# Soft mixture of experts in one long kernel: combine weights transposed during the experts, and expert outputs stored by expert

## The reference

```python
xn = _l2norm(x, axis=2)
phin = scale * _l2norm(phi, axis=0)
logits = jnp.einsum('bmd,dnp->bmnp', xn, phin)
d = jax.nn.softmax(logits, axis=1)
c = jax.nn.softmax(logits.reshape(b_, m_, n_ * p_), axis=-1).reshape(b_, m_, n_, p_)
xs = jnp.einsum('bmd,bmnp->bnpd', xn, d)
h = jax.nn.gelu(jnp.einsum('bnpd,ndh->bnph', xs, w1) + b1[None, :, None, :], approximate=False)
ys = jnp.einsum('bnph,nhd->bnpd', h, w2) + b2[None, :, None, :]
y = jnp.einsum('bnpd,bmnp->bmd', ys, c)
```

## Time and profile before

| | us |
|---|---|
| median of 3 runs | 1000.62 |
| lowest, highest | 994.01, 1002.33 |
| span of the profiled execution | 1013.5 |
| experts on TensorE, first matmul to the last | 275.11 to 454.14 |
| combine on TensorE, first transpose to the last product | 460.00 to 493.96 |
| PE busy in the span | 878.3 (87%) |
| DVE, ACT, POOL busy | 460.6, 315.7, 279.8 |

### The profile page before, as it was taken

How to read it: one execution, slowest core, us unless ns; L and a number is a source line. 1 busy time by engine, 2 the same in 40 slices (tenths; PEclk the granted TensorE clock), 3 DMA queues, 4 the chain that set the end, 5 groups by cost and what they waited for, 6 DMA issues and landing times. The chain is left out here.

```text
span 1013.5 us, 18267 instructions
## 1 busy us (share of the span) xinstructions
PE 878.3 (87%) x6209; PEld 626.3 (62%) x6209; DVE 460.6 (45%) x1542; ACT 315.7 (31%) x904; POOL 279.8 (28%) x242
## 2 busy tenths in 40 slices
PE   6789999889999989886898899977465999999980
PEld 6677888666556545454654677756462666666650
DVE  5764555538533322226653588845681222222220
ACT  2444333227533222221231566633101122211210
POOL 1440000000000000000232355530018188888454
PEclk9999999779899999998995799985556999999995
DMA  8999000000079999963500000001105255555222
GB/s 246 256 296 420 5 2 2 1 1 1 2 301 421 420 420 421 421 242 101 195 8 1 1 2 1 0 1 27 48 15 144 65 102 103 101 105 92 37 24 23
DMA packets 64454, 128.52 MB, mean 127 GB/s; under 512 B 26910, under 2 KB 47184, under 8 KB 54912
## 3 DMA queue, kind: packets, MB, share of 16 engines
q1 hardware_dynamic: 34432, 118.22, 32.4%
q0 software_dynamic: 29952, 9.36, 6.9%
HBM read 115.37 MB, written 11.98 MB: 126 GB/s over the span
## 5 line engine op out<-in xcount | busy, mean ns | idle before, releaser
L1805 POOL DMA_INDIRECT out_dram<-yr,put x48 | 105.7, 2202 | 65.6 <-issue 43.7
L1259 POOL MEMSET xg<- 96x74 f32 x1 | 0.2, 157 | 420.1 <-PE bank L1233 420.1
L1869 PE MATMUL bank<-zTa,w 128*128 128x372 f32 x256 | 90.2, 497 | 0.8 <-DVE zTb L1943 0.8
L1791 POOL DMA_INDIRECT zr<-z_rows,take x48 | 66.5, 1386 | 85.9 <-issue 85.9
L1952 DVE TENSOR_TENSOR hT<-sg,bank 128x372 f32<-128x372 f32 x64 | 31.8, 539 | 107.6 <-ACT sg L1913 63.1
L1093 DVE COPY eh<-bank 128x384 f32<-128x384 f32 x32 | 17.8, 557 | 119.1 <-PE bank L1129 119.1
L1869 PEld LDWEIGHTS bank<-zTa,w 128*128 128x128 f32 x256 | 47.5, 194 | 38.2 <-ACT sg L1913 8.4
L1151 PE MATMUL bank<-w2s,eg 128*64 128x192 f32 x768 | 69.4, 330 | 0.0
L1883 PE MATMUL bank<-w2r,hT 128*124 128x192 f32 x384 | 66.1, 330 | 0.8 <-DVE hT L1952 0.8
L1883 PEld LDWEIGHTS bank<-w2r,hT 128*124 128x124 f32 x384 | 61.9, 187 | 3.8 <-issue 3.8
L1913 ACT ACTIVATE sg<-bank 128x372 f32<-128x372 f32 x64 | 27.3, 478 | 115.6 <-PE bank L1874 115.6
(11 more groups left out here) (287 smaller groups left out, 1766.0 us busy)
## 6 DMA issues: line engine op xcount, KB each, us to landing
w1s<-in_w_dram SPq DMA_DIRECT2D x32, 1152.0 KB, 12.7
w2s<-in_w_dram SPq DMA_DIRECT2D x32, 1152.0 KB, 14.8
w<-in_w_dram SPq DMA_DIRECT2D x8, 1024.0 KB, 7.8
xt<-in_x_dram SPq DMA_DIRECT2D x22, 336.0 KB, 9.1
xT<-in_xT_dram SPq DMA_DIRECT2D x22, 333.0 KB, 8.3
ys<-eo SPq DMA_DIRECT2D x64, 48.0 KB, 10.0
w2r<-in_w2r_dram SPq DMA_DIRECT2D x8, 384.0 KB, 4.7
e<-ys SPq DMA_DIRECT2D x21, 96.0 KB, 2.0
```

The costliest lines, as they stand in the source:

```text
L1791: nc.gpsimd.indirect_dma_start(zr[b][:, j, :], None, z_rows, bass.IndirectOffsetOnAxis(ap=take[:, k:k + 1], axis=0), bounds_check=NROW - 1 ...
L1805: nc.gpsimd.indirect_dma_start(rows_out, bass.IndirectOffsetOnAxis(ap=put[:, k:k + 1], axis=0), yr[e % 2][:, j, :], None, bounds_check=OUT ...
L1869: nc.tensor.matmul(bank[to + 2 * part + half][:, 0:HS], w13[b][:, 0, at:at + 128], zTa[b][:, half * HS:(half + 1) * HS], start=True, stop= ...
```

## The change

Four things are altered together.

1. Spreading, transposing and copying the combine weights moves from combine into the experts loop. In steps 2 to 23, TensorE has two transposes more (`transpose_c`) behind `hidden`, ACT a copy of 128 x 222 (`keep_c`) behind `copy_h`, and DVE the spreading (`spread_c`) behind the bias. The transposed weights of all tiles are kept in a new buffer `cT`. The transposes go to the unused columns 256 to 477 of banks 6 and 7, whose columns 0 to 191 hold expert outputs. Therefore `output(p)` for p below 22 now waits for `keep_c(p)`, and `transpose_c(t)` waits for ACT's copy of pair t - 2.
2. `ys` is ordered by expert. A store writes one block of 64 rows for an expert. To make a tile's rows reachable, image g * 21 + t now belongs to tile t as its g-th image in `xy`, which only changes where ACT's copy in dispatch writes.
3. Combine reads `ys` in ten DMAs: three for tiles 0 to 2, three for tiles 3 to 11, four for the rest, into two of the former weight buffers each for `e1` and `e2`. The bias `b2` is laid out twelve times by the host and loaded in two DMAs that SP issues in its step 33, between the stores of pairs 28 and 29.
4. Combine on TensorE is the 22 times two products alone, over four PSUM banks, written out without a loop; DVE has the addition of tile t and then the statistics of tile t - 1; ACT has nothing.

```diff
@@ experts_act
+            def keep_c(t):
+                act.wait_ge(s_eT, t + 1)
+                nc.scalar.copy(cT[:, t], bank[6 + t % 2][:, 256:256 + 2 * TP].rearrange("p (c q) -> p c q", c=2)).then_inc(s_eTa, 1)
+
             for s in range(NPAIR + 2):
                 if s < NPAIR:
                     copy_h(s)
+                if 2 <= s < T + 2:
+                    keep_c(s - 2)
                 if 0 <= s - 1 < NPAIR:
                     gelu(s - 1)
@@ experts_pe
                 pe.wait_ge(s_dg, p + 1)
-                if p >= 2:
+                if p < T:
+                    pe.wait_ge(s_eTa, p + 1)
+                elif p >= 2:
                     pe.wait_ge(s_do, p - 1)
...
+            def transpose_c(t):
+                b = t % 2
+                pe.wait_ge(s_ecw, t + 1)
+                if t >= 2:
+                    pe.wait_ge(s_do, t - 1)
+                spread = cw[b][:].rearrange("p g n -> p (g n)")
+                nc.tensor.transpose(bank[6 + b][:, 256:256 + TP], spread[:, 0:128], ident[0:TP, 0:TP])
+                nc.tensor.transpose(bank[6 + b][:, 256 + TP:256 + 2 * TP], spread[:, 128:4 * NE], ident[0:TP, 0:TP]).then_inc(s_eT, 1)
+
@@ experts_sp
-                        sp.dma_start(ys_of[:, p + e * NPAIR, :], eo[b][e * B:(e + 1) * B]).then_inc(s_eo[b], 16)
+                        sp.dma_start(ys_of[p + e * NPAIR], eo[b][e * B:(e + 1) * B]).then_inc(s_eo[b], 16)
+                if s == NPAIR + 1:
+                    sp.wait_ge(s_dh, NPAIR - 1)
+                    for k in range(2):
+                        sp.dma_start(e2[k][NE:2 * NE], ins["b2"].rearrange("n (t d) -> n t d", d=ED)).then_inc(s_b2, 16)
@@ combine_sp
+            for k, (lo, hi) in enumerate(LOADS):
+                to = slice(lo % EB, lo % EB + hi - lo)
+                for g in range(2):
+                    sp.dma_start(e1[lo // EB][g * NE:(g + 1) * NE, to], rows(g, lo, hi)).then_inc(s_el[k], 16)
+                sp.dma_start(e2[lo // EB][0:NE, to], rows(2, lo, hi)).then_inc(s_el[k], 16)
+                if hi == T - 1:
+                    sp.dma_start(e1[1][0:NE, hi % EB], ys_of[:, B - 1, :]).then_inc(s_el[k], 16)
@@ combine_pe
+            def product(t):
+                k = [lo <= t < hi or t == hi == T - 1 for lo, hi in LOADS].index(True)
+                pe.wait_ge(s_el[k], 64 if k == len(LOADS) - 1 else 48)
+                if t >= 4:
+                    pe.wait_ge(s_h, 2 * T + t - 3)
+                else:
+                    pe.wait_ge(s_dc[t % 2], NPAIR)
+                nc.tensor.matmul(bank[t % 4][0:TP, 0:ED], cT[:, t, 0], e1[t // EB][:, t % EB, :], start=True, stop=False)
+                nc.tensor.matmul(bank[t % 4][0:TP, 0:ED], cT[:, t, 1], e2[t // EB][:, t % EB, :], start=False, stop=True).then_inc(s_ey, 1)
```

More of the change, by code:

```diff
@@ L46 @@
 PAIR = 2 * TP
+EB = 12
+LOADS = ((0, 3), (3, EB), (EB, T - 1))
 EX, EH = 8, 512
@@ L255, in tower @@
         cw = [sb(f"cw{b}", [TP, GB + 1, NE]) for b in range(2)]
-        e1 = [sb(f"e1{q}", [128, ED]) for q in range(4)]
-        e2 = [sb(f"e2{q}", [128, ED]) for q in range(4)]
-        c1 = [sb(f"c1{b}", [128, TP]) for b in range(2)]
-        c2 = [sb(f"c2{b}", [128, TP]) for b in range(2)]
+        cT = sb("cT", [128, T, 2, TP])
+        e1 = [w1s[q][:].rearrange("p (t d) -> p t d", d=ED) for q in (2, 3)]
+        e2 = [w1s[q][:].rearrange("p (t d) -> p t d", d=ED) for q in (4, 0)]
         close_scope()
@@ L426, in tower @@
         s_cxc = sem("expert_input_stored")
-        s_w1 = [sem(f"w1_in_then_expert_rows_in{q}") for q in range(RING)]
-        n_w1 = [16 * len(range(q, NPAIR, RING)) for q in range(RING)]
+        s_w1 = [sem(f"w1_in{q}") for q in range(RING)]
         s_w2 = [sem(f"w2_in{q}") for q in range(RING)]
@@ L438, in tower @@
         s_eT = sem("combine_transposed")
-        s_eTa = sem("combine_copied_act")
-        s_eTd = sem("combine_copied_dve")
+        s_eTa = sem("combine_weights_kept")
+        s_b2 = sem("expert_output_bias_in")
+        s_el = [sem(f"expert_rows_in{k}") for k in range(len(LOADS))]
         s_ey = sem("combine_product")
@@ L902, in store @@
                 for c in range(2):
-                    n = B - t * GB if isinstance(t, int) and t == T - 1 else GB
-                    last = nc.scalar.copy(xy[:, c, :, bass.ds(t * GB, n)].rearrange("p n g -> p g n"), p[:, c, 0:n])
+                    if isinstance(t, int) and t == T - 1:
+                        last = nc.scalar.copy(xy[:, c, :, B - 1:B].rearrange("p n g -> p g n"), p[:, c, 0:1])
+                    else:
+                        to = xy[:, c, :, 0:B - 1].rearrange("p n (g t) -> p g n t", g=GB)
+                        last = nc.scalar.copy(to[:, :, :, bass.ds(t, 1)].rearrange("p g n o -> p g (n o)"), p[:, c])
                 last.then_inc(s_cxc, 1)
@@ L1163, in combine_sp @@
         def combine_sp(sp):
-            for q in range(4):
-                sp.dma_start(e2[q][NE:2 * NE], ins["b2"]).then_inc(s_cbi, 16)
             for b in range(2):
                 sp.wait_ge(s_eo[b], 16 * NPAIR)
-            def load(t, q):
-                if after(t, 4):
-                    sp.wait_ge(s_ey, t - 3)
-                first = t * GB * NE
-                if isinstance(t, int) and t == T - 1:
-                    sp.dma_start(e1[q][0:NE], ys[first:first + NE]).then_inc(s_w1[q], 16)
-                else:
-                    sp.dma_start(e1[q][:], ys[bass.ds(first, 2 * NE)]).then_inc(s_w1[q], 16)
-                    sp.dma_start(e2[q][0:NE], ys[bass.ds(first + 2 * NE, NE)]).then_inc(s_w1[q], 16)
@@ L1180, in combine_sp @@
[L1180 to L1203 removed]
+            rows = lambda g, lo, hi: ys_of[:, g * (T - 1) + lo:g * (T - 1) + hi, :]
@@ L1225, in product @@
-            def product(t, q):
-                b = q % 2
-                pe.wait_ge(s_eTa, t + 1)
-                pe.wait_ge(s_eTd, t + 1)
-                pe.wait_ge(s_w1[q], 8 * (t - q) + n_w1[q] + (16 if isinstance(t, int) and t == T - 1 else 32))
-                if after(t, 2):
-                    pe.wait_ge(s_h, 2 * T + t - 1)
-                nc.tensor.matmul(bank[b][0:TP, 0:ED], c1[b][:], e1[q][:], start=True, stop=False)
-                nc.tensor.matmul(bank[b][0:TP, 0:ED], c2[b][:], e2[q][:], start=False, stop=True).then_inc(s_ey, 1)
@@ L1238, in value_columns @@
+            for t in range(T):
+                product(t)
         def value_columns(j):
@@ L1995, in _ @@
             experts_act(act)
-            combine_act(act)
             near_act(act)
```

55 lines of the change are left out of this document (20 added, 35 removed).

## The result

The kernel after the change takes 997.06 us (median of 20 runs, 989.65 to 1007.5), the one before 1003.69 (20 runs, 994.01 to 1013.94): ratio 0.9948, 95% interval 0.9924 to 0.9973. That is 5 us faster, between 3 and 8, and outside the forecast range. The two medians are 6.6 us apart; the ratio leaves out the runs that lie more than 1.5% above the fastest of their kernel, and comes out nearer to 1. Over those 20 runs the kernel before stands 3 us above the median of the three runs that the prediction had.

The account below looks back on a forecast made before the run. Experts were bound by PE, later by DMA; combine by a ring of transposes, copies and products. Terms -14.4 - 0.6 + 0.4 = -14.6 us took 1000.62 to 986 us; forecast 982 to 990, 8-in-10 range 977 to 994.

Parts of the forecast that it names:

- The pitch: Combine's products: 0.71 us a tile at the higher clock, between 0.65 and 0.82; with the low-clock intervals, 14.4 us saved.
- Combine, its start: Store landing and first ys loads before combine: first product at 460.9 instead of 461.46, 0.6 us saved; no fourth-tile wait.
- The rest, at nothing: Other parts cost nothing: DVE's spreading, bias loads between stores 28 and 29, ACT's last copy, stores, dispatch copy, near.
- The clock at its start: Start of combine: some 5.5 us at the lower clock, four intervals of 1.28 us, then 17 of 0.71.
- Rival B: Loads run at half rate (210 GB/s), delaying the fourth tile and ACT's last copy: 991 us; chance 0.11.
- The experts: Experts loop: PE-bound steps grow to 5.3 to 5.4 us, 0.4 us lost; the DMA-bound part loses nothing.
- the DMA's pace comes later, near step 19: Experts loop: steps reach the DMA's 5.85 us pace near step 19 or 20 rather than 13.
- The added wait: DMA-bound experts steps: output matmuls wait for keep_c, PE opens the next step 0.6 us late, without accumulating; nothing lost.
- rival A: Experts: the load queue runs dry and the delay adds up, 6.57 us a step, 1002 us; chance 0.05.
- The clock elsewhere (C): Behind combine: work moved forward against the granted clock, up or down by 8, 978 or 994 us; chance 0.16.
- D: Combine: the clock does not rise, 21 intervals of 1.28 us, 995.7 us; chance 0.06 together with E.
- E: Rival: DVE and PE alternate in combine, 996 us; 0.06 with D. In "behind E": end of the experts' last output matmul.

Follow-up runs that it names:

- e5: Kernel after, with the two bias loads into 64 partitions replaced by one load of the same bytes into 128 (wrong bias): ratio 0.9939 to the kernel before.
- e2: Kernel after, with the two long bias loads replaced by one short load that GpSimd copies out: ratio 0.9866 to the kernel before.
- e10: e2 with ys read back in seven short stretches of tiles in place of three: 984.87 us, ratio 0.9807 to the kernel before.
- e1: Kernel after, with the ys loads for e1's rows going into 128 partitions instead of 64 (wrong rows): ratio 0.9935 to the kernel before.
- e4: Kernel after, with spreading, transposing and keeping the weights moved behind the experts, before the first product: ratio 0.9894 to the kernel before.
- e11: e2 with six short stretches and images reordered so two of three image groups load into 128 partitions: ratio 0.9827 to the kernel before.
- e12: e11 plus 14 matmuls that nothing reads, ahead of the first product: ratio 0.983 to the kernel before.
- e6: e2 plus 14 matmuls that nothing reads, ahead of the first product: ratio 0.9888 to the kernel before.
- e9: e6 plus 10 more matmuls that nothing reads, ahead of the fourth tile: ratio 0.9845 to the kernel before.

## Why the prediction was wrong

**The pitch was right.** At the high clock 0.65 us a tile (463.83, 464.48), where I took 0.71 between 0.65 and 0.82. DVE's two instructions overlap and keep the same 0.65.

**The step that failed is "Combine, its start" together with "The rest, at nothing".** There the sum took 254 to 420 GB/s for transfers of `ys`, 420 for the bias and no wait of the fourth tile, and ACT's last copy was to wait for PE and not for a store. The choice went by the length of rows. The runs showed that here the partitions decide: the same rows of 9216 bytes went at 203 to 267 GB/s into 64 partitions and at 415 to 424 into 128 (e5). A third term was short as well: "The clock at its start" kept four intervals at the low clock, and had none behind a second wait.
- The first product was to come 0.6 us sooner and came 2.9 later. The first `ys` load is issued 6.1 us behind E (448.69 - 442.57), not 3.2, and the first stretch takes 4.1 from issue to product, not 3.6. e2, without the long bias loads, is at 7.05, so this half is shown to be the bias's.
- The 21 intervals were to take 17.2 us and took 20.8: the wait of the fourth tile, 3.17 (e10, with none, takes 15.5), and 1.0 for a low clock that came back behind it (5.7 intervals at 0.63 more, not 4), less 0.9 for the better pitch of the other 15 and 0.3 of small remainders on top. That the wait goes with shorter stretches is shown (e10). That the full rate would have removed it, as the sum had it, is not: e1, with two thirds of the bytes at 353 to 366 GB/s, still waited 2.62.

Together 3.5 + 3.6 us, and 0.6 from the experts: -6.9 in place of -14.6.

**Rival B was the right mechanism, with 0.11.** It had the two halves, the store behind the bias's loads and the fourth tile, and gave 4.6 us less gain; the trace has 7.1. ACT was held 3.2 us, not 1.7, and the return of the low clock was not in it, so its size was short by a third. The Trainium skill ("SBUF — State Buffer", section "Door 1: The DMA port swizzle") states the half bandwidth of a transfer to 64 partitions, and this trace agrees: 194 to 281 GB/s against 421. I weighed it as undecided for want of a row, and kept in the sum the rate of loads into twice as many partitions. The loads should have had the lower rate in the range at the least.

**The experts.** +1.0 measured, +0.4 forecast. The span is 179.0 before and 180.1 in e4, both without the transposes; with them it is 180.0 after and 179.1 to 180.1 in the other experiments, and 179.1 in e1, whose experts loop is that of the kernel after. So the +1.0 is not shown to be the change's. PE's step is 5.21 us (274.58 to 279.79) in the PE-bound part, where I had 5.3 to 5.4. That the DMA's pace comes later, near step 19, was wrong: step 13 takes 5.68 us (326.76 to 332.44), and from there to 390.90 a step takes 5.85 on the average, the pace of the loads. Only the place of the wait changed. It stands ahead of the output matmuls, for `keep_c` and so for the store ahead of it on ACT: 0.42 us at 330.47, 0.55 to 0.75 in the ten steps behind, 6.2 in all. The first wait for `w1s` comes in step 25, and the last, in step 31, is 0.59 (0.71 before). The added wait doesn't add up, which is why rival A fell.

**The clock elsewhere (C)** kept its place relative to the work: grant 0.50 from about 40 us behind the start of near in both kernels (before, 530 to 540 has a mean of 0.70, so the fall is near 534; after, 500 to 520 has 0.87, so near 515). D and E did not happen.

**The starting point.** 1000.62 was the median of three runs and 3 us low; the forecast of a difference of 14.6 was wrong by itself and does not need this.

## What to carry to other kernels

Before a few long transfers replace many short ones, count the partitions that each writes: by these runs transfers into 64 partitions went at 194 to 293 GB/s where the DMA share was about 1 or above, with rows of 1.5 to 9.2 KB, and transfers into 128 at 353 to 424, with rows of 6.9 to 9.2 KB (for the shorter rows into 128 in e11 and e12 no rate was read by itself). A store in the same queue behind such a load waits for it. Length also has a price of its own: a consumer waits for the last byte of its stretch, so the stretches should be as short as the consumer's head start is, and here seven of two to five tiles beat three of up to ten by 4.4 us with the same bytes at the same rate. When a rule of the Trainium skill speaks against a rate taken from a row that is only near, the forecast should stand on the lower of the two, or the range should.

## What the hardware showed unexpectedly

- The granted clock was 1.00 at 457 to 460 while PE did nothing, and 0.50 at 461 to 463 while it worked; it had worked from 452.79 to 457 and stood idle before and after. The grant did not follow the work at once. In e6 an idle 4.85 us was followed by 0.50 from about 462.4 to 465.8, and in e9, with that idle time filled, the grant stayed 1.00. So the wait for a load cost its length and then, at 0.63 us more a tile, 1.4 (e2) to 2.7 us (e5) of low clock.
- A DMA share of 1.0 to 1.2 with 200 to 267 GB/s: the share says that the engines are occupied, not that they move what they can.
- The kernel after and e10 are the same up to the end of the experts but for the load of the bias, and the first hidden matmul stands at 262.6 in one profile and at 274.0 in the other. A change of a stage of 30 us is better read from an event next to it than from the span.
